# Nine products of a constant tile between the first matmuls, and the first scaling of x ahead of a table load

## The reference

```python
scale = cond @ norm_w.T + 1.0                                   # 32 x 128, one row for a sequence
h = x * (scale[:, None, :] * rsqrt(mean(x * x) + EPS))
val, gate = split(h @ up_w.T, 2)                                # 128 -> 512 + 512
hq = act_quant(val * gelu(gate));  x = x + hq @ weight_quant(down_w).T
t = silu(cond @ W_t1.T + b_t1) @ W_t2.T + b_t2                  # of the second layer
modulations = silu(t + fside) @ W_c.T + b_c
```

## Time and profile before

| | |
|---|---|
| median of 3 runs | 317.65 us (317.05 to 318.71) |
| the profiled execution | 316.87 us, its span 315.1 us |
| PE busy | 278.0 us, 88% of the span |
| VectorE busy | 241.3 us, 77% |
| ACT, POOL busy | 189.1 us, 175.1 us |
| mean granted TensorE clock | 0.987 |

### The profile page before, as it was taken

One profiled execution on the slowest core, in us unless ns is written; L12 is line 12 of the kernel. 1 busy time (PEld: TensorE's weight loads), 2 busy tenths in 40 slices (PEclk: granted clock), 3 DMA queues, 4 the chain that ended last, 5 costly groups with the idle time before them and its releaser, 6 DMA issues.

```text
span 315.1 us, 8220 instructions
## 1 busy us (share of the span) xinstructions
PE 278.0 (88%) x2892; PEld 153.8 (49%) x2892; DVE 241.3 (77%) x642; ACT 189.1 (60%) x355; POOL 175.1 (56%) x357
## 2 busy tenths in 40 slices
PE   3989998798989576999999999988858999999993
PEld 2454554354445334656556565655434445554441
DVE  6579997767898985598989888898965686686432
ACT  4557987778787555587767777776554322333330
POOL 8032674976796669568778696943434444322300
PEclk9999999999999997799999999999999999999999
DMA  7950000430340003325353534520000011001112
GB/s 259 312 102 4 0 1 3 124 85 2 93 117 2 0 7 87 105 58 156 100 142 101 139 101 122 149 74 8 6 2 4 0 33 33 13 23 33 34 35 67
DMA packets 26217, 21.58 MB, mean 68 GB/s; under 512 B 4384, under 2 KB 25536, under 8 KB 25920
## 3 DMA queue, kind: packets, MB, share of 16 engines
q1 hardware_dynamic: 25744, 20.37, 24.4%
q10 hardware_dynamic: 432, 0.67, 0.6%
HBM read 4.26 MB, written 2.10 MB: 20 GB/s over the span
## 4 chain that ended last, share of the span: by engine, by line
PE 49%; DVE 18%; POOL 14%; issue 10%; ACT 5%; DMA 2%; SPq 1%; DVEq 0%; POOLq 0%; ACTq 0%
PE psum L274 42%; DVE mx L895 6%; POOL q_rest L1016 3%; POOL q_part L1018 2%; DVE hid L842 2%; DMA q_st<-q_part 1%; ACT sq L710 1%; POOL xn_tile L1071 1%; PE psum L623 1%; DVE projT L914 1%; DVE o_turn L902 1%; PE psum L460 1%; POOL q_part L1022 1%; ACT hrnd L717 1%; PE psum L535 1%
## 5 line engine op out<-in xcount | busy, mean ns | idle before, releaser
L895 DVE TENSOR_REDUCE mx<-psum 128x8 f32<-128x1024 f32 x64 | 75.3, 1192 | 12.7 <-PE psum L274 12.7
L736 ACT ACTIVATE probs<-psum 128x1024 f32<-128x1024 f32 x64 | 65.4, 1023 | 8.1 <-PE psum L274 6.6
L274 PE MATMUL psum<-w_early,h0T 128*128 128x512 f32 x128 | 69.4, 628 | 0.0
L771 ACT ACTIVATE g_act<-psum,w_late 128x512 f32<-128x512 f32 x32 | 22.0, 687 | 46.4 <-PE psum L274 46.4
L274 PE MATMUL psum<-probs,v_pad 128*32 128x128 f32 x1024 | 41.9, 283 | 3.3 <-DVE o_turn L902 2.8
L274 PE MATMUL psum<-h2T,w_late 128*128 128x512 f32 x64 | 31.3, 606 | 0.0
L274 PEld LDWEIGHTS psum<-probs,v_pad 128*32 128x32 f32 x1024 | 24.9, 110 | 10.8 <-ACT probs L736 4.4
L842 DVE SCALAR_TENSOR_TENSOR hid<-psum,rstd,gate 128x512 f32<-128x512 f32 x32 | 23.7, 741 | 8.0 <-PE psum L274 4.7
L274 PE MATMUL psum<-g_act,w_late 128*128 128x512 f32 x64 | 28.8, 592 | 0.0
L702 ACT ACTIVATE gate<-psum,rstd 128x512 f32<-128x512 f32 x32 | 22.0, 687 | 9.3 <-PE psum L274 8.9
L274 PE MATMUL psum<-q_st,k_st 64*128 64x128 bf16 x512 | 25.8, 221 | 0.7 <-DVE mx L895 0.5
(11 more groups left out here) (125 smaller groups left out, 545.9 us busy)
## 6 DMA issues: line engine op xcount, KB each, us to landing
q_st<-q_part SPq DMA_DIRECT2D x48, 128.0 KB
k_st<-k_part SPq DMA_DIRECT2D x48, 128.0 KB, 2.4
x_tok<-x SPq DMA_DIRECT2D x8, 256.0 KB, 7.5
out<-out_t SPq DMA_DIRECT2D x8, 256.0 KB, 2.3
w_late<-late SPq DMA_DIRECT2D x1, 1159.5 KB, 8.3
w_early<-early ACTq DMA_DIRECT2D x2, 256.0 KB, 4.8
k_st<-k_st SPq DMA_DIRECT2D x4, 128.0 KB, 5.8
q_st<-q_st SPq DMA_DIRECT2D x4, 128.0 KB
```

The costliest lines, as they stand in the source:

```text
L274: return nc.tensor.matmul(o, w, m, start=start, stop=stop, skip_group_check=shares)
L736: nc.scalar.activation(probs[:, n % 3, :, :, :].rearrange("p f j q -> p (f j q)"), psum[:, pair[0]:pair[1] + 1, :].rearrange("p a b -> p ( ...
L771: nc.scalar.activation(g_act[:, f, :], bank(2 + f % 2), ACT.Gelu_apprx_tanh, bias=wl("b_f1")[:, f:f + 1]).then_inc(c_gelu[f], 1)
L895: v.tensor_reduce(mx[:, c % 2, :, r, :], psum[:, pair[0]:pair[1] + 1, :].rearrange("p f (j k) -> p f j k", j=4), X_AXIS, ALU.max, negate=T ...
```

## The change

PE gets nine products of the tile `ones` with itself, fp32, 128 columns, which go to bank 5 and which nobody reads: three once the constants are written, ahead of the condition products; two ahead of the `t2` product; two ahead of the first transpose of x; two behind it. On ACT the first `scale_x` goes from behind the load of gelu's table to ahead of it.

```diff
+UNUSED_BANK = 5
@@ PE
+            def keep_at_work(n):
+                for _ in range(n):
+                    mm(bank(UNUSED_BANK)[:, 0:P], ones[:, :], ones[:, :])
+
+            pe.wait_ge(const_set, 6)
+            keep_at_work(3)
             pe.wait_ge(cond_loaded, 16)
             mm(bank(6)[:, 0:B], w_cond[:, B:B + D], w_cond[:, 0:B])
             mm(bank(6)[:, B:2 * B], w_cond[:, B + D:B + 2 * D], w_cond[:, 0:B]).then_inc(cond_mm, 1)
+            keep_at_work(2)
             pe.wait_ge(first_loaded, 16)
             pe.wait_ge(t1_set, 1)
             mm(bank(MISC_BANK)[:, 0:B], wf("t2"), t1[:, :]).then_inc(t2_mm, 1)
+            keep_at_work(2)
             transpose_x(0)
+            keep_at_work(2)
@@ ACT
             nc.scalar.activation(c_act[:, :], t2[:, :], ACT.Silu).then_inc(c_set, 1)
+            scale_x(0)
             nc.scalar.activation(warm[:, :], zero_c[:, :], ACT.Gelu)
-            scale_x(0)
```

## The result

By the ratio of the times, 0.9926 with a 95% interval of 0.9896 to 0.9955, the changed kernel is 0.74% faster, which on the 318.0 us that the kernel before took over 22 runs is 2.35 us. Over all 22 runs the change is not faster: its median is 319.42 us and its mean 318.8, against 318.0 and 317.9. The experiments give reasons to take the long runs for a part of what the change does, so the 2.35 us describe its nine shortest runs and not the kernel. The profiled execution, one of the nine, took 315.59 us (span 313.8), against 316.87 (span 315.1).

What follows compares the result with a forecast made beforehand. The prediction took the opening's chain of waits, then VectorE from the first hid, as the bound, with PE at half rate. An earlier h0T, nine products and an earlier clock rise gave 317.65 - 1.06 = 316.6 us, range 315.3 to 318.2.

Steps and rivals of the forecast that it cites:

- The bound of the opening: Opening to 17.00 us: a chain of waits through PE and ACT, then VectorE from 11.46; an earlier first hid moves the end.
- ACT's part: First h0T on ACT ahead of gelu's table load (1.28 us): alone, gate's first matmul from 7.73 to about 6.95, 0.78 us.
- The nine products: PE's opening: nine products take 4.2 us at half rate, gate's first matmul at 7.60 against 7.73, 0.13 us left.
- The cover on VectorE's t2: VectorE's opening: t2 product 0.3 us late, 0.36 us of cover before the squares, just enough.
- The rise: PE's clock in the opening: goes to full rate at 9.2 instead of about 13.4, first hid at 10.4 instead of 11.46.
- Rival 2: PE's opening: the products do not move the clock's rise, only 0.13 us gained, 317.5 us; chance 0.13.
- The sum: Whole kernel: the gain of 1.06 us carried to the end in full, median 317.65 - 1.06 = 316.6 us.
- rival 4: Mid-kernel: the half-rate stretch of 6.9 us goes, up to 3 us more gained, 313.6 us; chance 0.07.
- rival 3: PE's opening: the products take longer than the gaps, slower, up to 3.2 us late, 320.9 us; chance 0.05.
- What is late next: Behind the first hid: VectorE's operations to w_ternT at 17.00 move as one, so the gain reaches the end in full.

Runs made afterwards that it cites:

- E9: The changed kernel plus 24 products of ones in PE's later pauses: median 314.38 us, ratio 0.9907 to the kernel before.
- E11: The kernel before with ACT's move alone, without the nine products, plus 24 products in PE's later pauses: median 314.09 us, ratio 0.9912.
- E1: The kernel before with ACT's move alone, without the nine products: median 317.35 us, ratio 0.9965.
- E4: The changed kernel plus two memsets on VectorE, about 0.6 us, ahead of the first hid: median 320.3 us, ratio 1.0025 to the kernel before.
- E2: The kernel before with the nine products alone, ACT's order unchanged: median 320.62 us, ratio 1.0052.
- E10: The kernel before plus 24 products in PE's later pauses, neither ACT's move nor the nine products: median 315.18 us, ratio 0.9942.
- E5: The changed kernel plus seven products in PE's two pauses of steps 1 and 2: median 317.04 us, ratio 0.9948 to the kernel before.
- E8: The kernel before with ACT's move alone, plus seven products in steps 1 and 2 and twelve at the border to attention: median 315.31 us, ratio 0.9916.
- E7: The changed kernel plus seven products in steps 1 and 2 and twelve at the border to attention: median 314.88 us, ratio 0.9901 to the kernel before.

## Why the prediction was right, and where not

**The bound of the opening: right.** The chain did run through the first hid, and a gain there moved VectorE's stretch to w_ternT as one (0.60 and 0.60) and the end with it, once the clock holds (E9 to E11).

**ACT's part: right.** The forecast for the move alone was a gate's first matmul at 6.95; E1 shows 6.76. With the change, h0T's activation starts at 6.79 for 0.37 us and the load at 7.17, 0.01 us behind its end, with no drain ahead of it. The 1.28 us of the trace hold again, not the 2.66 that the Trainium skill gives (ScalarE: Activation LUTs, What ACT_TABLE_LOAD costs).

**The nine products: right in sum.** The gate's first matmul was put at 7.60 and stood at 7.61. Single terms were off both ways: from the second on, the instructions of the first three products start 0.21 us apart and not 0.233, while the condition products, whose load landed later in this run, started at 3.05 instead of 2.86. The cover on VectorE's t2 was just too short: 5.65 instead of 5.12, which moved the squares by 0.09 us, without effect.

**The rise: the mechanism half right, the size in range.** Put at 9.2, it came at 10.1 and 7.8 in the two traces of the change; the first hid, put at 10.4, at 10.86 and 9.71. The step that was wrong is the choice of what decides it: I let the rise hang on the products alone. E1 shows that ACT's move, by beginning step 0's work 0.97 us earlier, brings it forward too. Over the traces the products tend to bring the rise earlier: 7.4 to 10.1 in the seven with them, 9.2 to 11.5 in the four with ACT's move without them, 12.8 and 13.4 in the two with neither; the first two ranges overlap, and one kernel's rise scatters by over 2 us. But the products delay the gate's first matmul by 0.85 to 1.34 us. The two cancel: the first hid averages 10.11 in the five traces of the whole change (E4 aside), 10.13 in the four of ACT's move. Rival 2, that the products do not move the rise, is not borne out: with them alone it came at 9.5 (E2).

**The sum: a gain of 1.06 us for a measured 2.35.** The opening's share is 0.60 and 1.75 in traces, and with the clock held up (E10 to E9) 0.9 by the spans and 0.80 by the medians, so that term stands. The term that is missing is the half-rate stretches, which the sum put at nothing and rival 4 at a chance of 0.07. I treated them as one fixed place that the program might slip past. They come and go between kernels and between runs of one kernel; filling PE's pauses is worth 1.8 us in the kernel before by E10's ratio, 2.4 by the medians (317.59 and 315.18). That the ratio came out faster by more than the opening's share is in part luck: it is the figure of nine of 22 runs, and over all of them the median is 1.42 us above that of before, a loss that rival 3 alone allowed for, by a cause, products too long for the gaps, that the traces do not show. That the change's short runs meet fewer half-rate stretches isn't shown either: its two traces hold 13.7 and 10.2 us at half rate, that of the kernel before 6.8.

**What I did not see: what an early rise lays bare.** A pause of 0.27 us became one of 1.34, because PE got faster and VectorE did not. What is late next was answered for VectorE's chain; it was not asked what the idle engine's own clock does. E2's trace shows the price, a half-rate stretch at 16.4, and E5 that filling the two pauses ends the change's times above 319 (twelve runs, to 318.54).

**What stays open.** How much of the 2.35 us comes of leaving the long runs out; why ACT's move alone, with the same two pauses (1.34 and 1.07 in its trace), has no time above 318.82 in twelve runs; why the clock falls behind a pause in one execution and not in the next; and whether the change's long times are all the stretch at 16.4, as no trace of such a run of the change was taken. The granted clock of these 13 runs, 0.952 to 0.968, agrees with it, though a mean does not say where: E2's and E4's traces, which have the stretch, show 0.962, the change's own two 0.978 and 0.982.

## What to carry to other kernels

Ask of products that only keep PE busy where they stand: ahead of the critical work they delay it by their own length, and here a reorder on ACT alone brought the same first hid, without the long runs; in the pauses behind it they cost little (up to 0.4 us in E10) and held the clock in most runs. When an engine gets faster, list the pauses that it gains, and what its clock does behind them. Before taking a small gain apart, look at the granted clock over the whole span: holding it up in mid-kernel was worth 1.8 us here, the change's opening 0.8. And look at all runs: a change that lengthens some of them can seem faster by the others.

## What the runs showed of the hardware

- The instant at which TensorE's clock rises scatters between executions of one kernel: 10.1 and 7.8 us for the change, with the gate's first matmul at 7.61 in both. The Trainium skill (TensorE: Matmul & The Clock Gate, What's actually happening) says that it differs from run to run, and these two traces agree.
- A clock at full rate fell behind short pauses of PE with work between them: behind 1.34 and 1.08 us in E2 (16.4), behind 1.82 in the kernel before, behind 1.6 at projT in E8 (228.4), behind 0.48 and 0.76 in E7 (205.4). The length of a pause does not settle it: none of the 13 traces shows a fall behind the pause of 1.67 us at 61 to 67 us (63.02), and the kernel before shows none behind 1.73 at 229.4. Once down the clock stayed there for 3.4 to 10.2 us, also under PE work with hardly a pause (10.03 busy of 10.20 us in E2).
- With 24 products of a constant tile in PE's pauses, 0.22 us each at full rate (in E5 their instructions start 0.11 apart), the clock stood at its upper level from the rise to 300 us in three traces (E9 to E11); the granted clock of their other runs goes from 1.000 down to 0.981.
- The view by stretches prints a granted clock of 1.00 ahead of the first change of level, where the spacing of 0.855 us shows the lower one.
